# Graph attention block on one core: the row maximum placed beside the folded sums, and the reciprocal of the row sum kept in PSUM

## The reference

```python
h = jnp.maximum(_layernorm(x, axis=-1), 0.0)
# _L0_gnn_ref(h, adj, adj, Wq, Wk, Wv, Wo):
q = split_heads(x @ Wq.T)
k = split_heads(x @ Wk.T)
v = split_heads(x @ Wv.T)
bias = (spatial_encoding + edge_encoding)[:, None]
a = jnp.einsum('bhnd,bhmd->bhnm', q, k) * scale + bias
row_nonzero = jnp.any(a != 0, axis=-1, keepdims=True)
a = jnp.where(row_nonzero, a, -jnp.inf)
p = jax.nn.softmax(a, axis=-1)
p = jnp.where(jnp.isnan(p), 0.0, p)
o = jnp.einsum('bhnm,bhmd->bhnd', p, v)
return o @ Wo.T
x = x + _L0_gnn_ref(...)
```

## Time and profile before

| | us |
|---|---|
| median of three runs | 1376.79 |
| span of the profiled execution | 1374.0 |
| PE busy | 1302.3 (95%) |
| PEld busy | 1230.5 (90%) |
| DVE busy | 1260.6 (92%) |
| ACT busy | 1041.4 (76%) |
| POOL busy | 1015.0 (74%) |

### The profile page before, as it was taken

The page is one execution under the profiler, slowest core; times in us unless marked ns, Lnnn a source line. Parts: engine busy times, 40 slices in busy tenths (PEclk is TensorE's granted clock), DMA queues, the critical chain, the costliest instruction groups (busy, mean ns, idle before and its releaser), DMA issues. The chain is left out here.

```text
span 1374.0 us, 44286 instructions
## 1 busy us (share of the span) xinstructions
PE 1302.3 (95%) x13072; PEld 1230.5 (90%) x13072; DVE 1260.6 (92%) x4279; ACT 1041.4 (76%) x2379; POOL 1015.0 (74%) x1519
## 2 busy tenths in 40 slices
PE   5999999999999999999999999999999999999996
PEld 4889999999999999999999999999999999999985
DVE  6999999999999999999999999999999999999995
ACT  3777778777778777787777787777787777787784
POOL 5777777777778777777777777777777777777775
PEclk9999999999999999999999999999999999999997
DMA  6435444445344445354454454354454454444441
GB/s 214 110 92 139 107 121 122 118 119 136 100 130 115 115 129 123 104 140 115 106 138 115 107 142 112 105 145 106 116 127 117 115 137 104 125 116 120 108 119 43
DMA packets 90772, 163.88 MB, mean 119 GB/s; under 512 B 14976, under 2 KB 23168, under 8 KB 90752
## 3 DMA queue, kind: packets, MB, share of 16 engines
q1 hardware_dynamic: 90752, 163.64, 46.0%
HBM read 46.14 MB, written 16.78 MB: 46 GB/s over the span
## 5 line engine op out<-in xcount | busy, mean ns | idle before, releaser
L855 POOL TENSOR_TENSOR fold<-minus 128x512 f32<-128x512 f32 x256 | 329.0, 1285 | 249.3 <-DVE minus_max L698 249.3
L549 ACT ACTIVATE probs<-minus,minus_max 128x256 f32<-128x256 f32 x1024 | 461.5, 500 | 58.2 <-DVE minus_max L698 58.0
L559 ACT ACTIVATE pT_hi<-pT_ps 128x512 f16<-128x512 f32 x512 | 306.1, 598 | 150.9 <-PE pT_ps L397 149.1
L698 DVE CUSTOM_DVE_ANT_0 minus<-s_ps,adj_now 128x256 f32<-128x256 f32 x1024 | 388.7, 415 | 21.9 <-PE s_ps L386 16.2
L716 DVE TENSOR_TENSOR pT_lo<-pT_ps,pT_hi 128x512 f16<-128x512 f32 x512 | 348.4, 680 | 58.0 <-ACT pT_hi L559 57.8
L397 PE MATMUL pT_ps<-ident,probs 128*128 128x128 f32 x2048 | 308.9, 273 | 1.3 <-ACT probs L549 1.3
L324 PE MATMUL job_ps<-hT_hi,w_hi 128*128 128x256 f32 x1024 | 299.4, 292 | 3.4 <-DVE hT_lo L666 2.9
L324 PE MATMUL job_ps<-hT_lo,w_hi 128*128 128x256 f32 x1024 | 289.2, 282 | 0.0
L324 PE MATMUL job_ps<-hT_hi,w_lo 128*128 128x256 f32 x1024 | 288.7, 282 | 0.0
L397 PEld LDWEIGHTS pT_ps<-ident,probs 128*128 128x128 f32 x2048 | 241.3, 141 | 15.1 <-ACT probs L549 2.4
L386 PE MATMUL s_ps<-qk_stack 96*128 96x256 f32 x1024 | 247.7, 324 | 2.1 <-DMA qk_stack<-qk_parts 2.0
(11 more groups left out here) (82 smaller groups left out, 2651.0 us busy)
## 6 DMA issues: line engine op xcount, KB each, us to landing
qk_stack<-qk_parts SPq DMA_DIRECT2D x768, 128.0 KB, 2.3
x_in<-x SPq DMA_DIRECT2D x32, 512.0 KB, 3.4
x_res<-x SPq DMA_DIRECT2D x32, 512.0 KB, 3.6
out<-y SPq DMA_DIRECT2D x64, 256.0 KB, 2.1
adj_in<-adj SPq DMA_DIRECT2D x32, 256.0 KB, 3.5
minus<-wq_t SPq DMA_DIRECT2D x2, 512.0 KB, 5.0
qk_parts<-wv SPq DMA_DIRECT2D x2, 512.0 KB, 8.7
y<-wk_t SPq DMA_DIRECT2D x1, 512.0 KB, 6.7
```

Of the source, the lines that this page charges most:

```text
L549: end = nc.scalar.activation(probs[hh % 2][:, t, :], minus[hh // 2 % 2][:, hh % 2, t, :], ACT.Exp, bias=minus_max[:, hh // 2 % 4, hh % 2, ...
L559: nc.scalar.activation(pT_hi[hh % 4][:, :, :], pT_ps[hh % 2][:, :].rearrange("p (m n) -> p m n", m=NT), ACT.Copy).then_inc(pT_high, 1)
L698: end = nc.vector.tensor_tensor_reduce(out=minus[pair % 2][:, hh % 2, t, :], in0=s_ps[SCORE_BANK[hh]][:, t * N:(t + 1) * N], in1=adj_now[: ...
L855: nc.gpsimd.tensor_tensor(f1[:, :, :], src[:, :, 0:N // 2], src[:, :, N // 2:N], ALU.add).then_inc(folded1, 1)
```

## The change

The row minimum of the negated scores (the bias of the exponential) moves from `minus_max` into the last column of a wider tensor `bounds`, whose other 32 columns take the folded sums of the same row. One reduction (maximum of absolute values over 33 columns) then tests both, and L734 is gone. The reciprocal of the row sum reads the sum where TensorE left it, in PSUM, and writes its result to an unused column of the same bank (`FREE`). The last step then has one operand in SBUF and one in PSUM, and comes ahead of `low_probs` instead of behind it. As the bank `o_ps` is now read by that last step, TensorE's `values` waits for `factor_ready` where it waited for `o_copied`; the counts are the same.

```diff
+    FREE = 3 * HD
-        minus_max = sb("minus_max", [P, 4, 2, NT])
+        BOUND = N // 8
+        bounds = sb("bounds", [P, 4, 2 * NT, BOUND + 1])
-        fold3 = [sb(f"fold3_{i}", [P, 2 * NT, N // 8]) for i in range(2)]
-        some = [sb(f"some{i}", [P, 4, 2 * NT]) for i in range(2)]
+        some = [sb(f"some{i}", [P, 2 * NT]) for i in range(2)]
+        factor = [sb(f"factor{i}", [P, 2 * NT]) for i in range(2)]
+        o_sums = o_ps[:, :].rearrange("p (q c) -> p q c", c=P)
@@ values (TensorE)
-                    pe.wait_ge(o_copied, b * PAIRS + hh // 2)
+                    pe.wait_ge(factor_ready, b * PAIRS + hh // 2)
@@ exponentials (ScalarE)
-                                               bias=minus_max[:, hh // 2 % 4, hh % 2, t:t + 1], scale=-1.0)
+                                               bias=bounds[:, hh // 2 % 4, 2 * (hh % 2) + t, BOUND:BOUND + 1],
+                                               scale=-1.0)
@@ shift (VectorE)
-                        accum_out=minus_max[:, pair % 4, hh % 2, t:t + 1])
+                        accum_out=bounds[:, pair % 4, 2 * (hh % 2) + t, BOUND:BOUND + 1])
@@ VectorE
-            def factor1(b, pair):
+            def any_nonzero(b, pair):
                 dve.wait_ge(folded3, b * PAIRS + (pair + 1))
-                nc.vector.tensor_reduce(some[pair % 2][:, 0, :], fold3[pair % 2][:, :, :], AX_X,
-                                        ALU.add).then_inc(some_ready, 1)
+                nc.vector.tensor_reduce(some[pair % 2][:, :], bounds[:, pair % 4, :, :], AX_X, ALU.max,
+                                        apply_absolute_value=True).then_inc(some_ready, 1)
                 dve.wait_ge(o_copied, b * PAIRS + (pair + 1))
-                nc.vector.reciprocal(some[pair % 2][:, 1, :], o_raw[pair % 2][:, :, ONES]).then_inc(rcp_ready, 1)
-            def factor2(b, pair):
+                nc.vector.reciprocal(o_sums[:, :, FREE], o_sums[:, :, ONES]).then_inc(rcp_ready, 1)
+            def factors(b, pair, early):
                 dve.wait_ge(some_ready, b * PAIRS + (pair + 1))
-                nc.vector.scalar_tensor_tensor(some[pair % 2][:, 2, :],
-                                               minus_max[:, pair % 4, :, :].rearrange("p h t -> p (h t)"), 0.0,
-                                               some[pair % 2][:, 0, :], ALU.not_equal, ALU.max).then_inc(keep_ready, 1)
-            def factor3(b, pair, early):
                 dve.wait_ge(rcp_ready, b * PAIRS + (pair + 1))
-                dve.wait_ge(keep_ready, b * PAIRS + (pair + 1))
                 if not early:
                     dve.wait_ge(o_ready, b * PAIRS + (pair - 1))
-                nc.vector.scalar_tensor_tensor(some[pair % 2][:, 3, :], some[pair % 2][:, 2, :], 0.0,
-                                               some[pair % 2][:, 1, :], ALU.not_equal,
-                                               ALU.mult).then_inc(factor_ready, 1)
+                nc.vector.scalar_tensor_tensor(factor[pair % 2][:, :], some[pair % 2][:, :], 0.0,
+                                               o_sums[:, :, FREE], ALU.not_equal, ALU.mult).then_inc(factor_ready, 1)
@@ body (VectorE)
-                        factor1(*pair)
+                        any_nonzero(*pair)
                     for kind, n, d in ended_before(hh, first, last):
                         take(kind, n, b + d)
                     if pair:
-                        factor2(*pair)
+                        factors(*pair, first and hh < 6)
                     low_probs(b, hh, first and hh < 2)
-                    if pair:
-                        factor3(*pair, first and hh < 6)
@@ divide, fold (GpSimd)
-                    some[pair % 2][:, 3, :].rearrange("p (h t) -> p h t", h=2).unsqueeze(3).to_broadcast([P, 2, NT, HD]),
+                    factor[pair % 2][:, :].rearrange("p (h t) -> p h t", h=2).unsqueeze(3).to_broadcast([P, 2, NT, HD]),
-                f1, f2, f3 = fold1[pair % 2], fold2[pair % 2], fold3[pair % 2]
+                f1, f2, f3 = fold1[pair % 2], fold2[pair % 2], bounds[:, pair % 4, :, 0:BOUND]
```

More of the change, by code:

```diff
@@ L192, in attention_block @@
         folded2, folded3 = sem("folded2"), sem("folded3")
-        some_ready, keep_ready = sem("some_ready"), sem("keep_ready")
-        rcp_ready, factor_ready, o_ready = sem("rcp_ready"), sem("factor_ready"), sem("o_ready")
+        some_ready, rcp_ready = sem("some_ready"), sem("rcp_ready")
+        factor_ready, o_ready = sem("factor_ready"), sem("o_ready")
         o_added = sem("o_added")
@@ L792, in _ @@
             body(B - 1, False, True)
-            factor1(B - 1, PAIRS - 1)
-            factor2(B - 1, PAIRS - 1)
-            factor3(B - 1, PAIRS - 1, False)
+            any_nonzero(B - 1, PAIRS - 1)
+            factors(B - 1, PAIRS - 1, False)
             take("o", 1, B - 1)
@@ L863, in fold @@
                     pool.wait_ge(some_ready, b * PAIRS + (pair - 1))
-                nc.gpsimd.tensor_tensor(f3[:, :, :], f2[:, :, 0:N // 8], f2[:, :, N // 8:N // 4],
+                nc.gpsimd.tensor_tensor(f3, f2[:, :, 0:N // 8], f2[:, :, N // 8:N // 4],
                                         ALU.add).then_inc(folded3, 1)
```

## The result

The changed kernel takes 1319.98 us (median; 1317.2 to 1320.4) beside 1376.89 us of the kernel before: a ratio of 0.9581, 95% interval 0.9567 to 0.9594. The span of the profiled execution went from 1374.0 to 1317.9.

The account below looks back on a forecast made before the run. The loop was taken as bound by TensorE's own 40.1 us a turn plus one 1.43 us wait for VectorE. Gains of 41.5 + 1.2 + 3.2 + 3.9 = 49.8 us gave 1327 us, range 1320 to 1348.

Parts of the forecast that it names:

- the hole: TensorE's slot 2, each loop turn: 1.43 us standing still between the values of heads 0 and 1, for VectorE's low part.
- What holds VectorE up: Slots 15 and 1: a VectorE instruction with two SBUF inputs stands until GpSimd's running instruction ends; L734 1134 ns against 132.
- The factor step: VectorE, ahead of the low part: with one SBUF operand it never stretches, 130 to 200 ns, 0.07 us to the next start.
- The chain in slot 1: VectorE, from reduction to low part start: 1.37 us becomes 0.20 + 0.20 + 0.07 = 0.47, so 0.90 earlier.
- What is handed on from slot 15: VectorE: the low part of head 15 starts 0.73 us earlier and `shift` of head 2 0.93, passed on to slot 1.
- the feared case: Rival: something such as `pT_hi` of head 0 holds VectorE between slots 15 and 1, half the hole stays; 1346 us, chance 0.14.
- The cover: Slot 2: TensorE wants head 1's low part at 620.19 and gets it at 619.79, so 0.40 us to spare.
- The sum of the loop: 29 turns: 29 x 1.43 = 41.5 us for the hole and 29 x 0.11 = 3.2 us for slot 0's small gap.
- a tie: Slot 4: GpSimd's h would be ready about when TensorE transposes it; counted 0, bounded by 0.1 us a turn (3 us).
- The two ends: Batches 0 and 31: 3.9 us gained, with 2 and 8 as bounds; the first loop turn adds 1.2.
- the lock stays: Rival: the factor step still waits for GpSimd and takes L734's place and its 1.05 us; about 1370 us, chance 0.07.
- Slower: Rival: the PSUM steps cost c more per pair, the full hole back at c = 1.83; 1397 us at 2.5, chance 0.04.

Follow-up runs that it names:

- the first run: The changed kernel with the reciprocal read from o_raw and kept in SBUF, so the factor step has two SBUF operands: 1347.61 us, ratio 0.9788.
- the seventh run: The kernel before with GpSimd's folds and VectorE's reduction halved, the other half of each row left out of the test: 1333.19 us, ratio 0.9681.
- the second run: The kernel before with only reciprocal and last step over PSUM, L734 kept, TensorE's values waiting for factor_ready: 1366.7 us, ratio 0.9931.
- the ninth run: The kernel before with six useless TensorE products in each of slots 6 to 11 of batch 31: 1373.8 us, ratio 0.9986.

## Why the prediction was right, and where it missed

The mechanism was right; two terms of the sum were too small. The step that failed is the term for batch 0 and batch 31: with the first turn it stood at 5.1 us and measured 8.6. The loop stood at 44.7 and measured 47.4. With the median 2.1 us above the span instead of 2.8, that makes the 7 us between 1327 and 1319.98. Of the three, any one as forecast would have left the time inside the range, so on which side of its end it fell by 0.02 us is chance; that the sum was 7 us off is not.

*What bounds the kernel, and the hole:* right. TensorE's own work is the turn, and the 1.43 us hole closed in every turn.

*What holds VectorE up:* right, shown from both sides by the first and the seventh run. It holds for these small steps; the copy of the adjacency, with one input in SBUF, is stretched too (last section).

*The factor step:* right in kind. It takes 142 to 159 ns and never stretches.

*The chain in slot 1:* mis-sized. From reduction to low part it is 597.02 - 596.33 = 0.69 us, not 0.47. Reciprocal to factor is 0.38 for 0.20, and factor to low part 0.11 for 0.07. Since the same 0.37 stands in the first run, with the reciprocal in SBUF, PSUM is not its cause. The reciprocal in PSUM takes 180 ns against 166. The argument that had put the read from PSUM at nothing proved nothing: a rate and a fixed part were drawn from two durations, 678 ns and 0.28 us, and any two fit such a line. The value came out right all the same. The Trainium skill's figure (Perfetto Trace Analysis, Optimizing Scalar/DVE Operations), from which 0.13 us for both steps was estimated, is not seen: 14 ns on the reciprocal, and the last step with one operand in PSUM takes 140 to 159 ns in the second run, where the same step in SBUF has a minimum of 146.

*What is handed on from slot 15:* the feared case came true in part, and another term was missing. Measured from the transposes of head 0 (614.15 and 591.96), `shift` of head 2 starts 1.32 earlier (1.33 after them before, 0.01 now), where 0.93 was counted. Slot 15 gives 0.99 of it: 0.73 for L734 as counted, 0.26 behind the low part for 0.20 (591.97 - 591.19 = 0.78 for 1.04). The other 0.33 VectorE brings along from the slots before, as in the first run. Then the low part of head 0 waits 0.23 us for `pT_hi`, and of the 1.32 the reduction of slot 1 has 0.99 left (4.37 for 5.36). That 0.93 came out so nearly is luck: one part was left out and another cut it back.

*The cover:* 0.11 was to spare instead of 0.40. The chain is 0.22 longer, less 0.06 that more was handed on. And TensorE wants the low part 0.12 earlier, since its slot 0 is shorter: the prediction had that gain in the sum and not in the cover. The hole still closed.

*The sum of the loop:* forecast 29 x 1.54 = 44.7, measured 47.4. The hole is 1.43 as forecast. Missing is mainly the bank wait behind it, 0.14 a turn, which I could have seen in the 13 products that took 1.77 us instead of 1.63. It was too short for the view of waits. Against it stand 0.08 a turn for h, which I had called a tie and bounded by 0.1. Slot 2 as a whole gives 1.59 and slot 0 gives 0.12 for 0.11.

*The two ends:* forecast 5.1 with the first turn, measured 2.4 + 6.2. This is the larger of the two misses. I had taken batch 31 by its booked waits alone, although the granted clock of that stretch is in the windows. Part of its 6.2 us is TensorE's clock: before, it fell in the stretch where TensorE idled, and six products of the output then ran from 1349.36 to 1352.07, 2.71 us, for 1.46 in the changed kernel; the ninth run, with VectorE's program as before, gets some 1.6 us back. Another 0.9 lies behind the transposes of the last head (18.49 to 17.57), and varies as much between two executions of one program, so it is not shown to be the change's. The remaining 3.7 is left for VectorE's pace in batch 31 (slots 8 and 10 of TensorE are 0.8 and 1.0 shorter, and VectorE was busy all of 1340 to 1350), which was not measured by itself. At the other end, 3.4 us are gained from slot 4 of batch 0 (its transposes of h) to slot 4 of the first loop turn (40.77 to 37.37); the stretch ahead of slot 4 of batch 0, which the change hardly touches, is 1.0 longer (46.2 to 47.2), and goes from 44.8 to 49.2 us over the 14 traces. Its cause stays open.

*The range:* its lower end was the forecast with the ends at 8 us "and a little more": 2.9 us for everything else. The ends took 8.6 and the loop 2.7.

*The rivals:* "the lock stays" had its mechanism right and its size wrong by 22 us (1370 for 1347.6 in the first run). The reduction of slot 1 came 0.78 earlier instead of 0.24: the step behind the low part costs 0.44 with the loop's branch, and 0.33 is brought along from the slots before. "Slower" put the return of the full hole at 1.83 us more; the run with 1.8 us more is still 22 us faster than before, since part of it falls into waits.

## What to carry to other kernels

A small VectorE instruction whose duration varies while its shape does not may be waiting inside itself, as L734 did. Look for the other engine's instruction that ends with it, and look first at the few places where it stands in front of what the bounding engine waits for. When such a stall goes, the gain can be larger than its booked waits: here shorter waits hid behind it, and the clock of the idle TensorE had dropped at the end. And the next late step, here h, was already in the old trace, with little cover.

## What the runs showed of the hardware that I had not expected

- A dependent pair of small VectorE instructions is 0.20 us apart in the prologue, but reciprocal and factor are 0.37 to 0.38 apart in slot 1 of the loop turns, in PSUM and in SBUF alike, and 0.28 in slots 7 to 13 of the changed kernel (in the others a take stands between). Why the three differ was not tried.
- The copy of the adjacency (SBUF to SBUF, one input) took 414 to 575 ns in the kernel before and 568 to 911 ns in the changed one. It is stretched as well, although it has one SBUF input, and who comes first matters. In the kernel before one copy starts at 568.05, as a fold ends (568.10), and takes 0.41; the fold that starts at 568.18, while it runs, takes 0.59, where the median of its line (L864) is 0.458. In the changed kernel one starts at 546.65, behind a fold that began at 546.53, and takes 0.91. The Trainium skill (SBUF — State Buffer, Who interferes with whom) lists such copies among those that can take the shared pair, if their operands meet the conditions of a two-port mode; the trace agrees. It costs nothing here, as its 14.3 us of waiting is off TensorE's way.
- Useless products on an idle TensorE went with a kernel 1.8 us shorter (1373.8 for 1375.6 us, ratio 0.9986 with an interval that ends at 0.9996, so barely clear of no change). The granted clock of the stretch is the difference that the windows show.
